# Second-batch codes left as 1024 + code, written by ScalarE alone, and new queue orders for nine tiles

## The reference, cut to what matters

```python
# x: (2, 1024, 2048) fp32; ctx: (2, 2048, 2048) fp32; s, z: scale and zero point of each side
def fake_quant(v, s, z):
    return (clip(round(v / s + z), 0, 255) - z) * s
x = x + tanh(g_xattn) * matmul(fake_quant(layernorm(x), s1, z1), fake_quant(ctx, s2, z2))
# then 4 experts of rank 16, the best two kept per token
h = layernorm(x)
logits = h @ Wr.T                  # (tokens, 4)
gates = softmax(top 2 of logits)
delta = sum_e gates[e] * (h @ A[e].T) @ B[e].T * 4
x = x + tanh(g_ffn) * delta
```

## Time and profile before

| | us |
|---|---|
| Median of 3 runs | 376.11 (375.16 to 376.32) |
| The profiled execution | 376.49 |
| Its span in the trace | 374.7 |
| Busy: TensorE / its weight loads | 337.6 / 188.7 |
| Busy: VectorE, ScalarE, GpSimd | 290.2, 251.0, 96.8 |
| DMA | 69.17 MB, mean 185 GB/s |

### The profile page before, as it was taken

How to read it: one execution, slowest core, us unless ns; L and a number is a source line. 1 busy time by engine, 2 the same in 40 slices (tenths; PEclk the granted TensorE clock), 3 DMA queues, 4 the chain that set the end, 5 groups by cost and what they waited for, 6 DMA issues and landing times. The chain is left out here.

```text
span 374.7 us, 6441 instructions
## 1 busy us (share of the span) xinstructions
PE 337.6 (90%) x2372; PEld 188.7 (50%) x2372; DVE 290.2 (77%) x715; ACT 251.0 (67%) x207; POOL 96.8 (26%) x107
## 2 busy tenths in 40 slices
PE   0579989999985789999989999999999999999984
PEld 0234434445653665455555556464656565555552
DVE  4785889589996799999947796968686877866685
ACT  1769848949999699689898147464747473756150
POOL 3100430005545322033043222140505050505000
PEclk9999999999998599999999999999999999999999
DMA  7999999960046769672570524141405020202023
GB/s 218 415 420 419 420 420 420 417 278 2 3 148 239 268 247 359 213 260 87 172 258 1 193 107 152 56 170 57 170 34 192 2 115 1 114 0 114 0 86 140
DMA packets 19185, 69.17 MB, mean 185 GB/s; under 512 B 2256, under 2 KB 2256, under 8 KB 19024
## 3 DMA queue, kind: packets, MB, share of 16 engines
q1 hardware_dynamic: 19152, 68.73, 48.4%
HBM read 51.94 MB, written 16.78 MB: 183 GB/s over the span
## 5 line engine op out<-in xcount | busy, mean ns | idle before, releaser
L671 PE MATMUL ps_main<-q,q1T 128*128 128x512 f16 x832 | 197.4, 379 | 2.2 <-ACT q1T L460 1.6
L671 PEld LDWEIGHTS ps_main<-q,q1T 128*128 128x128 f16 x832 | 77.4, 98 | 87.2 <-issue 9.0
L446 ACT ACTIVATE c_code<-q,small_tile 128x1024 uint8<-128x1024 f32 x62 | 74.7, 1239 | 25.0 <-DVE q L1139 13.7
L470 ACT ACTIVATE h_parts<-xr,small_tile 128x2048 f16<-128x2048 f32 x15 | 31.4, 2094 | 39.4 <-DVE small_tile L1217 39.4
L390 POOL TENSOR_TENSOR h_parts<-work,h_parts 128x512 f16<-128x512 f32 x30 | 34.8, 1180 | 66.3 <-ACT work L476 66.3
L1139 DVE TENSOR_SCALAR q<-c_code,small_tile 128x1024 f16<-128x1024 f16 x64 | 37.0, 580 | 14.0 <-ACT c_code L446 13.6
L1200 DVE SCALAR_TENSOR_TENSOR xr<-ps_main,small_tile,xr 128x512 f32<-128x512 f32 x52 | 38.6, 743 | 8.1 <-PE ps_main L671 8.0
L1144 DVE BATCH_NORM_STATS2 small_tile<-xr 128x6 f32<-128x512 f32 x64 | 40.9, 680 | 5.2 <-DMA xr<-in_x 5.2
L1205 DVE BATCH_NORM_STATS2 small_tile<-xr 128x6 f32<-128x512 f32 x64 | 43.6, 687 | 0.9
L1273 DVE TENSOR_TENSOR xr<-ps_delta,xr 128x512 f32<-128x512 f32 x62 | 41.2, 680 | 3.9 <-PE ps_delta L756 3.2
L381 POOL TENSOR_TENSOR small_tile<-small_tile 128x1 f32<-128x1 f32 x16 | 9.3, 583 | 128.3 <-DVE small_tile L1213 128.3
(11 more groups left out here) (122 smaller groups left out, 415.1 us busy)
## 6 DMA issues: line engine op xcount, KB each, us to landing
q<-in_ctx SPq DMA_DIRECT2D x62, 512.0 KB, 10.9
xr<-in_x SPq DMA_DIRECT2D x32, 512.0 KB, 4.9
out_x<-xr SPq DMA_DIRECT2D x30, 512.0 KB, 3.4
h_parts<-in_B SPq DMA_DIRECT2D x1, 1024.0 KB, 16.5
q1T<-in_ctx SPq DMA_DIRECT2D x2, 512.0 KB, 6.4
out_x<-xr SPq DMA_DIRECT2D x4, 256.0 KB, 2.3
xr<-in_A SPq DMA_DIRECT2D x1, 544.0 KB, 16.2
small_tile<-in_params SPq DMA_DIRECT2D x1, 3.0 KB, 2.6
```

The costliest lines, as they stand in the source:

```text
L446: nc.scalar.activation(c_byte[:, i % 2, :], stage(i), ACT.Identity, bias=par[:, 3:4], scale=inv_s[:, 1:2]).then_inc(row_scaled, 1)
L470: nc.scalar.activation(h_hi[:, :], xr[:, b % RING, :], ACT.Identity, bias=h_bias[:, b % 2:b % 2 + 1], scale=h_rstd[:, b % 2:b % 2 + 1]).th ...
L671: mm = pe.matmul(product_bank(b, n)[:, :], q1T_of(b)[:, k, :], q2[:, batch(b), k, cols(n)], start=(k == 0), stop=(k == KT - 1))
```

## The change

1. The codes of batch 1 stay as 1024 + code. `clear(k)` on GpSimd fills the place of block k (2048 float16 elements, written as 1024 float32 elements whose two halves both read 1024), and ScalarE writes the row's bytes there directly. There is no `code_row` from row 32 on, and TensorE waits for ScalarE's row. Block k of batch 1 has place `slot_of[k]` in `q2`, so that staging places are given up in an order; `left_by[k]` is the number of rows scaled after which the place is empty. A staging place is added in `c_code`, free once 32 rows are coded.
2. The products of tiles 8 to 15 then contain (1024 + zero point) times the sum of the tile's own codes per row. ScalarE sums these (`sum_codes`, two per tile), VectorE makes the shift from them (`shift_of_row`), and `add_delta` of these tiles subtracts it with a three-operand instruction.
3. New orders on all five queues up to tile 8.

```diff
-UNITS = 17
+UNITS = 18
+TWO_BASES = 9.473556003354462e+21
-        late_unit = (8, 9, 10, 11, 12, 13, 14, 15, 16, 13, 14, 15, 14, 15, 15, 16)
-        unit_of = [i % KT for i in range(3 * KT)] + list(late_unit)
+        late_unit = (0, 1, 2, 3, 4, 5, 6, 7, 16, 17, 0, 1, 2, 3, 4, 5, 16, 17, 0, 1, 2, 3, 16, 17, 0, 1, 16, 17, 16, 17, 16, 17)
+        unit_of = [i % KT for i in range(2 * KT)] + list(late_unit)
+        slot_of = (8, 9, 10, 11, 12, 13, 14, 15, 7, 6, 5, 4, 3, 2, 1, 0)
+        left_by = (25, 26, 27, 28, 29, 30, 31, 32, 40, 40, 48, 48, 54, 54, 58, 58)
...
                 elif unit_of[i] == UNITS - 1:
                     sp.wait_ge(main_done, parts_done(3, 3))
+                elif unit_of[i] == UNITS - 2:
+                    sp.wait_ge(row_coded, 2 * KT)
...
+            def clear(k):
+                pool.wait_ge(row_scaled, left_by[k])
+                nc.gpsimd.memset(q2_pair[:, slot_of[k], :], TWO_BASES).then_inc(place_cleared, 1)
...
             def scale_row(i):
                 act.wait_ge(row_loaded[unit_of[i]], 16 * (unit_turn(i)[1] + 1))
-                wait(act, row_coded, i - 1)
-                nc.scalar.activation(c_byte[:, i % 2, :], stage(i), ACT.Identity,
+                batch_of, k, h = place(i)
+                if batch_of == 0:
+                    wait(act, row_coded, i - 1)
+                    byte = c_byte[:, i % 2, :]
+                else:
+                    act.wait_ge(place_cleared, k + 1)
+                    byte = q2_byte[:, slot_of[k], half(h), 0]
+                nc.scalar.activation(byte, stage(i), ACT.Identity,
...
             def scale_x(b):
                 wait(act, q1_turned, b)
+                wait(act, codes_summed, 2 * (b - PER_B))
...
+            def sum_codes(b):
+                act.wait_ge(x_scaled, b + 1)
+                wait(act, row_summed, b - PER_B)
+                for h in range(2):
+                    wait(act, codes_summed, 2 * (b - PER_B) + h)
+                    nc.scalar.activation(byte_copy[:, :], x_byte[:, half(h)], ACT.Identity, bias=0.0, scale=1.0,
+                                         accum_out=code_sums[:, h:h + 1]).then_inc(codes_summed, 1)
...
-                        pe.wait_ge(row_coded, 2 * KT + 2 * k + n // 2 + 1)
+                        pe.wait_ge(row_scaled, 2 * KT + 2 * k + n // 2 + 1)
...
+            def shift_of_row(b):
+                dve.wait_ge(codes_summed, 2 * (b - PER_B) + 2)
+                nc.vector.scalar_tensor_tensor(out=row_sum[:, :], in0=code_sums[:, 0:1], scalar=code_sums[:, 1:2], in1=x_zeros[:, :],
+                                               op0=ALU.add, op1=ALU.add).then_inc(row_summed, 1)
+                dve.wait_ge(row_summed, b - PER_B + 1)
+                nc.vector.tensor_scalar(shift[:, b % RING:b % RING + 1], row_sum[:, :], code_gain[:, :], None, ALU.mult).then_inc(shift_ready, 1)
...
-                nc.vector.tensor_tensor(x1, src[:, :], x1, ALU.add).then_inc(out_ready, 1)
+                if b < PER_B:
+                    nc.vector.tensor_tensor(x1, src[:, :], x1, ALU.add).then_inc(out_ready, 1)
+                else:
+                    dve.wait_ge(shift_ready, b - PER_B + 1)
+                    nc.vector.scalar_tensor_tensor(out=x1, in0=src[:, :], scalar=shift[:, b % RING:b % RING + 1], in1=x1,
+                                                   op0=ALU.subtract, op1=ALU.add).then_inc(out_ready, 1)
```

More of the change, by code:

```diff
@@ L105, in build @@
         low_centre = small(1)
+        code_gain = small(1)
+        x_zeros = small(1)
+        code_sums = small(2)
+        row_sum = small(1)
+        shift = small(RING)
         rest = small(2)
@@ L406, in _ @@
             split_a()
+            clear(0)
+            clear(1)
+            clear(2)
             power_x(4)
+            clear(3)
+            clear(4)
             power_h(0)
[L409 to L412, removed]
+            clear(5)
+            clear(6)
+            low_part(0, 0)
+            power_h(1)
+            low_part(0, 1)
+            power_h(2)
+            low_part(1, 0)
+            low_part(1, 1)
+            clear(7)
+            low_part(2, 0)
+            low_part(2, 1)
+            power_h(3)
+            low_part(3, 0)
+            clear(8)
             power_x(5)
+            low_part(3, 1)
+            clear(9)
+            power_h(4)
             low_part(4, 0)
+            clear(10)
+            low_part(4, 1)
+            clear(11)
             power_x(6)
-            low_part(4, 1)
+            clear(12)
             power_h(5)
@@ L419, in _ @@
             low_part(5, 0)
+            clear(13)
+            clear(14)
+            power_x(8)
+            clear(15)
+            power_h(6)
             low_part(5, 1)
-            power_x(8)
+            low_part(6, 0)
             power_x(9)
[L423 to L426, removed]
+            low_part(6, 1)
+            power_h(7)
+            low_part(7, 0)
+            low_part(7, 1)
             for b in range(STEADY, TILES):
@@ L905, in program @@
[L905 to L913 removed]
+                delta(0, 0)
+                main(4, 1, general, 7, 9)
+                delta(0, 1)
+                turn_lo(1, 1)
+                delta(0, 2)
+                main(4, 1, general, 9, 10)
@@ new lines, in program @@
+                turn_hi(6, 0)
+                main(7, 2, general, 4, 7)
+                turn_hi(6, 1)
+                main(7, 2, general, 7, 12)
+                turn_q1(8, 5)
+                main(7, 2, general, 12, 16)
+                main(7, 3, general, 0, 2)
+                mid_hi(6, 0)
+                main(7, 3, general, 2, 5)
+                turn_lo(6, 0)
+                main(7, 3, general, 5, 6)
+                turn_gate(5, 9)
+                main(7, 3, general, 6, 16)
+                main(8, 0, general, 0, 1)
@@ L1390, in _ @@
-            add_delta(0, 1)
             copy_loT(1)
-            add_delta(0, 2)
-            bias_h(3)
             add_delta(0, 3)
             rank_gates(1)
-            code_row(40)
+            stats_h(4, 0)
+            weigh(1)
+            add_main(4, 1)
+            split_gate(1)
+            copy_loT(2)
+            bias_h(3)
+            rank_gates(2)
+            add_delta(1, 0)
+            add_delta(1, 1)
+            stats_x(5, 0)
+            weigh(2)
+            stats_x(5, 1)
@@ L1426, in _ @@
+            add_main(5, 0)
             stats_x(6, 0)
-            add_delta(2, 3)
-            weigh(3)
+            add_main(5, 1)
             stats_x(6, 1)
```

802 lines of the change are left out of this document (384 added, 418 removed).

## The result

The changed kernel takes **359.29 us** (358.96 to 359.61, median of 4 runs) against 376.22 us for the kernel before on the same chip (375.16 to 376.65, 4 runs): ratio 0.9554, 95% interval 0.9532 to 0.9576, or 16.9 us less. Its profiled execution is 358.96 us with a span of 357.1. The forecast was 363.8, range 357.5 to 371: right in sign and inside the range, 4.5 us too high.

The account below looks back on a forecast made before the run. TensorE was taken as the limit, with 14.6 us lost in the hole. Tile 5 at 118.3 + 79.8 + 1.4 + 4 gave 203.5 against 216.05: gain 12.55 less 0.25, so 376.11 - 12.3 = 363.8 us, range 357.5 to 371.

Parts of the forecast that it names:

- The start: Loads up to tile 1: row 2 becomes unit 8, first product moves from 18.85 to 20.1, tile 1 about 28.0, 1.3 waited.
- Tiles 0 to 4: First product to tile 5's first: TensorE alone 116.1, but x of tile 5 arrives late, so 118.3 against 136.29 before.
- tiles 5 to 8: Stage to tile 9: old 79.8 plus 1.4 added work gives 199.5, plus 4 charged for closer handovers: 203.5.
- the hole: Stretch 110.63 to 136.29 before tile 5's first product, TensorE busy 16.33 of 25.66 us; 14.6 us lost there.
- Costs named as covered: ScalarE's sums, 2.3 us per tile, and VectorE's added work, 0.65 per steady tile: free; only the last tile's +0.25 bare.
- Clears: 16 GpSimd fills of 1024 float elements, 0.9 us each by elements, 14 us in all, nothing charged.
- The rival of clears against code rows: Clears 0 to 2 meet code rows 24 to 30, 2.7 to 5.4 us, shifting tile 0 onward: 366 to 369; chance 0.10.
- The relief: 32 of VectorE's 64 code operations go, 18.6 us; 7.5 leave the stretch 82 to 131 where it held TensorE up.
- TensorE alone decides: Rival: slips below 1 us, x of tile 5 in time; tile 5 at 116, tile 9 196 to 198, 356 to 358; 0.12.
- VectorE still holds tiles 1 to 3 back: Rival: x of tile 5 some 5 us later, clock lowered, half of 14.6 us remains: 368 to 372; chance 0.18.
- The relief is empty: Rival: ScalarE's rows wait for clears as they did for codings, order gives nothing: 375 to 377; chance 0.03.
- Slower: the last rows: Rows 54 to 63 share four places, 7.6 us a turn; two slipped turns give 15 us, 378 to 380; chance 0.07.

Follow-up runs that it names:

- old_order: The changed kernel's new codes, clears, sums and shifts with the five queue lists of the kernel before, six clears ahead of tile 4's power; 378.04 us, ratio 1.0077.
- new_order_old_codes: The changed kernel's lists, but batch 1 coded by VectorE as before, without clears, sums and shifts, places assigned anew; 373.90 us, ratio 0.9962.

## Why the prediction was right, and where it was off

**The start** was right to some tenths: first product 20.1 forecast, 20.07 measured, behind row 2, which ScalarE starts to scale at 15.99 as soon as it is there (forecast 16.1); tile 1 28.0 and 28.60; the wait ahead of it put at 1.3, measured 0.95.

**Tiles 0 to 4.** The chain was right step by step. Forecast and measured: scale_x(4) done 74.4 and 75.65; tile 0's low copy 84.8 and 84.37; statistics of x of tile 5 from 108.4 to 110.8 and from 107.77 to 111.2; tile 5's first product **118.3 and 118.44**. This is ScalarE's timeline where the chain ends:

```profile
113.11 2.10 ACT L514 ACTIVATE x_byte<-xr,small_tile 128x2048 uint8<-128x2048 f32 x1 [0.25 <-DVE small_tile L1251]
115.11 0.99 ACT L558 COPY hT<-ps_turn 128x1024 f16<-128x1024 f16 x1
...
116.33 1.97 ACT L531 ACTIVATE q1T<-ps_gate,small_tile 128x2048 f16<-128x2048 uint8 x1 [0.23 <-PE ps_gate L724]
```

ScalarE's list and the round trip of x of tile 5 meet as worked out, 2 us behind the 116.1 that TensorE's own work would allow. That is why the sum held although each had its own error of about 1 us.

**The step that failed** is the size of one term in tiles 5 to 8: "I charge 4 for the closer one (bounds 0 and 10): 203.5". Measured is 198.35, and the drift is nil. The charge came from the 7 us that the old list lost in 92 us ahead of the hole (the earlier trace rows give 5.5 of idle time there), but those gaps lie where rows arrive; the earlier trace rows themselves show 1.4 us of TensorE's idle time in 79.76 for tiles 5 to 8, and the new list has 79.91 - 78.96 = 0.95. The "2.3 of waits" for that stage is a misreading too: it takes in the 1.26 that end at 136.29, where the stage begins. The nearer row was the one to go by. Another 1.3 us came from the 1.4 of added work, of which TensorE shows only 0.6 (78.96 against 78.38). Together that is the whole miss between 203.5 and 198.35.

**Costs named as covered.** The sums are (ScalarE's timeline of the changed kernel in the steady stage):

```profile
236.25 1.04 ACT L523 ACTIVATE byte_copy<-x_byte 128x1024 uint8<-128x1024 uint8 x1
237.19 0.19 ACT L523 ACTIVATION_READ_ACCUMULATOR byte_copy<-x_byte 128x1 f32 x1
237.41 1.06 ACT L523 ACTIVATE byte_copy<-x_byte 128x1024 uint8<-128x1024 uint8 x1
...
241.60 2.09 ACT L541 ACTIVATE h_parts<-xr,small_tile 128x2048 f16<-128x2048 f32 x1 [3.03 <-DVE small_tile L1309]
```

From one start to the next 1.16, taken 1.13; ScalarE still waits 3.03 behind them, and twice the load cost nothing. The three-operand add_delta takes 743 ns, as taken. The row sum is not quite tiny (275 ns in the mean, once 0.73 us), and the steady 19.75 us per tile stand: right.

**Clears.** 0.95 us each, 0.9 forecast: the fill goes by elements. Their groups, with the codings that are left:

```profile
L420 POOL MEMSET q<- 128x1024 f32 x16 | 15.1, 953 | 17.9 <-ACT q L507 9.3 <-ACT c_code L507 8.6
```

```profile
L1223 DVE TENSOR_SCALAR q<-c_code,small_tile 128x1024 f16<-128x1024 f16 x32 | 18.9, 597 | 4.2 <-ACT c_code L507 4.0
```

The rival of clears against code rows is right in its mechanism, and nearly in its price; what it had wrong is that the lost time would reach TensorE. In old_order a coding that begins with a clear takes 1.26 us, the ones before and after it 0.47 (VectorE's timeline; the clear is at 64.16 for 0.95):

```profile
63.11 0.47 DVE L1200 TENSOR_SCALAR q<-c_code,small_tile 128x1024 f16<-128x1024 f16 x1
64.14 1.26 DVE L1200 TENSOR_SCALAR q<-c_code,small_tile 128x1024 f16<-128x1024 f16 x1
66.50 0.47 DVE L1200 TENSOR_SCALAR q<-c_code,small_tile 128x1024 f16<-128x1024 f16 x1
```

This agrees with the Trainium skill (SBUF — State Buffer, on the shared port pair): whichever of a two-port VectorE operation and a GpSimd operation starts first holds the pair for its whole length. Which of the two came first here can't be read, as they begin within 0.02 us of each other. In the changed kernel only clears 0 to 2 (at 55.52, 57.06 and 58.19) meet codings, and the two pairs of codings beside them take 1.0 and 1.5 us more than the last two, which stand alone (VectorE's timeline):

```profile
54.90 1.86 DVE L1223 TENSOR_SCALAR q<-c_code,small_tile 128x1024 f16<-128x1024 f16 x2
57.03 2.42 DVE L1223 TENSOR_SCALAR q<-c_code,small_tile 128x1024 f16<-128x1024 f16 x2 [0.28 <-ACT c_code L507]
...
65.66 0.87 DVE L1223 TENSOR_SCALAR q<-c_code,small_tile 128x1024 f16<-128x1024 f16 x2
```

That is 2.5 us in all, close to the 2.7 at the lower end of what the rival charged. It did not pass on: VectorE still stood 0.19 us for x of tile 4 at 62.64, and row 31 is coded at 65.66 + 0.87 = 66.5 (forecast 67.8).

**The relief.** "7.5 us leave the stretch in which it held TensorE up" is where the argument was weak. VectorE was nearly full there, but the relief alone brought tile 5 forward by 1.6 us and the kernel by nothing. Releasers in a timeline name the last link (VectorE's copy, 3.81 us in the earlier trace rows); the length of the stretch was ScalarE's list. The sum did not suffer, since it was made from the new list and not from the relief. "Most of the rest leaves 136 to 195 ..., worth nothing by itself" holds for the old order (0.999); in the new one 11.4 us of idle load put back in that stretch cost 4.

**The rivals.** "TensorE alone decides" asked for tile 5 at 116, and x of tile 5 kept it at 118.44 as argued; its tile 9 (196 to 198) was nearly reached all the same. "VectorE still holds tiles 1 to 3 back" did not come. "The relief is empty" is false for the whole change, but true of the relief in the old order. "Slower: the last rows" did not come: from 118.44 to 198.35 the only wait besides the first is 0.78 us for VectorE's add of a product, none for a row.

**Open.** What the relief is worth in the new order beyond the 6 us up to tile 5: new_order_old_codes with places that don't hold x of tile 7 back was not run. Whether x of tile 5 could come sooner by another slot was not tried, nor what holds the kernel without fillers at 117.05.

## What to carry to other kernels

In a hole where several engines are nearly full, count the work that each has in its list between two handovers that the critical engine needs (here ScalarE's two operand copies) before believing the releaser in the timeline. Relieving an engine and reordering the lists were worth 0 and 1.4 us by the totals, and together 17; but the totals mislead. By stages the order alone had closed the hole and lost the time again at one load that waited for its place. So part a change in two, but compare the halves stage by stage, and ask of each new wait whether the experiment itself made it. And a charge for drift belongs to the stage in which it was seen; take it from the nearest stage's idle time.

## What was not expected of the hardware

A VectorE operation can be held up by several GpSimd instructions in a row: of the float16 TENSOR_SCALARs of 512 elements, at a median of 353 ns, one stood for 2900 ns beside three GpSimd instructions that followed each other, two of them plain fills. A fill on GpSimd is thus no harmless neighbour. An accumulator output on ScalarE adds a separate read of 0.19 us to an activation of 1.05 us. And leaving out eight matmuls that kept TensorE busy for 1.9 us at the start made the kernel 1.35 us faster, with the granted clock unchanged.
